# The end of a graph layer and LSTM kernel: last rows gated singly, sums on TensorE, the check between the output pieces

## The reference

```python
x = x + relu(adj @ (item @ W_item.T + b_item) + layernorm(x) @ W_user.T + b_user)   # adj 10000 x 10000
h = lstm(layernorm(x))                      # one sequence of 10000 steps, hidden size 128
g = argmax(h @ W_lin.T + b_lin, -1)         # 0 or 1 for every step
w = g * h
inc = cumsum(w, over steps); prefix = inc - w; suffix = inc[last] - inc
out = x + 2*h + prefix*fw_att + suffix*bw_att
```

## Time and profile before

| quantity | value |
|---|---|
| median of 3 runs | 1538.49 us (1537.8 to 1540.41) |
| profiled execution, its own time | 1538.81 us |
| its span | 1537.0 us |
| mean granted TensorE clock | 0.985 of full |
| busy TensorE / VectorE / ScalarE / GpSimd | 96% / 78% / 70% / 13% |
| DMA bytes | 426.73 MB |

### The profile page before, as it was taken

How to read it: one execution, slowest core, us unless ns; L and a number is a source line. 1 busy time by engine, 2 the same in 40 slices (tenths; PEclk the granted TensorE clock), 3 DMA queues, 4 the chain that set the end, 5 groups by cost and what they waited for, 6 DMA issues and landing times.

```text
span 1537.0 us, 25512 instructions
## 1 busy us (share of the span) xinstructions
PE 1471.3 (96%) x7890; PEld 1251.9 (81%) x7890; DVE 1201.8 (78%) x2018; ACT 1083.2 (70%) x1581; POOL 193.2 (13%) x172
## 2 busy tenths in 40 slices
PE   6999999999999999999999999999999899999991
PEld 5887887887887887887887887787787799999991
DVE  5998888888888888888888887887887456566667
ACT  4677777777777777777777777777776455556661
POOL 0000000000000000000000000000000000046765
PEclk9999999999999999999999999999999899999996
DMA  9789999999999999999999999999997300000003
GB/s 373 274 307 371 353 345 371 353 343 371 353 344 371 351 346 371 353 344 370 352 346 370 353 343 362 354 341 369 353 346 277 141 0 0 0 1 0 0 0 134
DMA packets 70080, 426.73 MB, mean 278 GB/s; under 512 B 8674, under 2 KB 17698, under 8 KB 69540
## 3 DMA queue, kind: packets, MB, share of 16 engines
q1 hardware_dynamic: 68320, 425.12, 73.1%
q10 hardware_dynamic: 1732, 1.24, 0.3%
HBM read 416.09 MB, written 10.24 MB: 277 GB/s over the span
## 4 chain that ended last, share of the span: by engine, by line
issue 77%; PE 20%; DVE 1%; POOL 0%; ACT 0%; POOLq 0%; DVEq 0%
PE psZ L729 9%; PE psZ L739 9%; PE psZ L745 1%; DVE y L1146 1%; POOL rstd L381 0%; POOLq L384 0%; DVE cum L1069 0%; ACT normed L492 0%; DVE cum L1067 0%; PE psV L639 0%; DVE dif L1057 0%; DVE dif L1054 0%; ACT u L506 0%; DVE y L1140 0%; DVE dif L1059 0%
## 5 line engine op out<-in xcount | busy, mean ns | idle before, releaser
L863 DVE TENSOR_TENSOR a_lo<-raw,a_hi 128x1000 fp32r<-128x1000 f32 (+1 forms) x800 | 907.4, 1180 | 139.6 <-ACT a_hi L521 136.1
L521 ACT ACTIVATE a_hi<-raw 128x1000 fp32r<-128x1000 f32 (+1 forms) x800 | 803.9, 1029 | 204.3 <-PE psG L664 185.6
L662 PE MATMUL psG<-a_hi,item_hi 128*128 128x500 f32 (+1 forms) x1580 | 637.0, 403 | 17.5 <-DVE a_lo L863 17.4
L664 PE MATMUL psG<-a_hi,item_lo 128*128 128x500 f32 (+1 forms) x1580 | 616.5, 390 | 0.0
L663 PE MATMUL psG<-a_lo,item_hi 128*128 128x500 f32 (+1 forms) x1580 | 613.6, 388 | 0.0
L662 PEld LDWEIGHTS psG<-a_hi,item_hi 128*128 128x128 f32 (+1 forms) x1580 | 297.0, 188 | 98.6 <-DVE a_lo L863 28.8
L664 PEld LDWEIGHTS psG<-a_hi,item_lo 128*128 128x128 f32 (+1 forms) x1580 | 298.1, 189 | 61.4
L663 PEld LDWEIGHTS psG<-a_lo,item_hi 128*128 128x128 f32 (+1 forms) x1580 | 298.0, 189 | 61.1 <-issue 4.4
L381 POOL TENSOR_TENSOR rstd<-var,minus_half 125x4 f32<-125x4 f32 x40 | 74.3, 1859 | 1119.4 <-DVE var L847 1119.4
L729 PE MATMUL psZ<-u,wx 128*128 (+1 forms) x1280 | 158.0, 277 | 1.6 <-POOL u L389 1.6
L729 PEld LDWEIGHTS psZ<-u,wx 128*128 128x128 f32 x1280 | 154.4, 194 | 3.6 <-issue 2.0
(11 more groups left out here) (111 smaller groups left out, 575.9 us busy)
## 6 DMA issues: line engine op xcount, KB each, us to landing
raw<-in_adj_main SPq DMA_DIRECT2D x360, 1000.0 KB, 5.7
raw<-in_adj_main SPq DMA_DIRECT2D x40, 750.0 KB, 4.1
x_copy<-xb SPq DMA_DIRECT2D x20, 250.0 KB, 5.2
x<-x_copy SPq DMA_DIRECT2D x1, 5000.0 KB, 15.5
out<-y SPq DMA_DIRECT2D x25, 200.0 KB, 2.4
xb<-in_xT SPq DMA_DIRECT2D x18, 250.0 KB, 5.4
u<-in_itemT SPq DMA_DIRECT2D x3, 1024.0 KB, 18.7
u<-in_itemT SPq DMA_DIRECT2D x1, 904.0 KB, 24.0
```

What stands on the lines that cost most here:

```text
L521: nc.scalar.activation(a_hi[:, s % CUT, 0:n], raw[:, r % RAW, at:at + n], ACT.Copy)\
L662: pe.matmul(bank, w_hi, hi, start=(c == 0), stop=False)
L664: last = pe.matmul(bank, w_lo, hi, start=False, stop=(c == CH))
L863: dve.tensor_tensor(a_lo[:, s % CUT, 0:n], raw[:, r % RAW, at:at + n], a_hi[:, s % CUT, 0:n].bitcast(f32), ALU.subtract).then_inc(lo_ready, 1)
```

## The change

The last pair of rows (38 and 39) is taken out of GpSimd's `sums`. Each of the two rows is gated by itself (`gate_row`). TensorE adds up, with identity and diagonal matrices as weights, what makes up their `y`: hist, x1 and dfb times the running sum, in PSUM banks 0 and 3; and in bank 1 the totals of every chunk (running sum before the pair plus the two gated rows). VectorE adds mbw times the gated row and writes the row of `y` (`last_y`). `cum` is made from the totals in PSUM. The shift is made twice: by VectorE into PSUM, which VectorE's pieces read, and by ScalarE into SBUF for GpSimd's. The check stands between piece 14 and piece 15 of the output; the head and piece 0 are last, and so is the store of piece 0; flag and branch come behind them. The branch now waits for all stores and writes the output anew from ScalarE's queue. A matrix `dfd` (dfb on the diagonal) is made once ahead of the LSTM.

```diff
-            for f in range(OUTS):                       # SyncE
+            for f in (*range(1, OUTS), 0):
...
-            with nc.gpsimd.Fori(PAIRS // 4 + 1, PAIRS // 2) as i:
+            with nc.gpsimd.Fori(PAIRS // 4 + 1, PAIRS // 2 - 1) as i:
                 sums(2 * i, 0)
                 sums(2 * i + 1, 1)
-            write_y(PAIRS - 1, 1)
-            pool.wait_ge(y_ready, PAIRS)
-            pool.wait_ge(shift_ready, 1)
+            sums(PAIRS - 2, 0)
+            pool.wait_ge(run_c_ready, PAIRS - 1)
+            write_y(PAIRS - 2, 0)
+            pool.wait_ge(y_ready, PAIRS - 1)
+            pool.wait_ge(last_rows, 2)
+            pool.wait_ge(shift_sb_ready, 1)
...
-            scale_gated(PAIRS - 1, 1)                   # ScalarE
-            scale_run(PAIRS - 1, 1)
+            act.wait_ge(total_ready, 1)
+            nc.scalar.activation(shift[:, :], cum[:, 0:K], ACT.Identity, scale=dfb[:, 0:1], bias=total[:, 0:1])
...
+            def add_up(w, columns, at, first=False, last=False):      # TensorE
+                return pe.matmul(psZ[:, SUM_BANK[at], 0:K], w[:, :], columns, start=first, stop=last, ...)
+            def add_total(columns, first=False, last=False):
+                return pe.matmul(psZ[:, TOT_BANK, 0:K], ident[:, :], columns, start=first, stop=last)
+            pe.wait_ge(t1_ready[0], STEPS)
+            pe.wait_ge(t1_ready[1], STEPS)
+            pe.wait_ge(run_ready, 2 * PAIRS - 1)
+            add_up(ident, hist[:, L - 2, :], 0, first=True)
+            add_total(run[:, 1, 0, :], first=True)
             pe.wait_ge(h_ready[0], STEPS)
             pe.wait_ge(h_ready[1], STEPS)
-            logits(L - 1, 1, 1)
+            pe.wait_ge(gated, PAIRS - 1)
+            logits(L - 1, 0, 0)
+            pe.wait_ge(gated, PAIRS)
+            add_total(gh[:, 1, 0, :])
+            pe.wait_ge(dfd_ready, 1)
+            add_up(dfd, run[:, 1, 0, :], 0)
+            add_up(ident, last_row(x1, L - 2), 0, last=True).then_inc(row_sums, 1)
+            pe.wait_ge(gated, PAIRS + 1)
+            add_total(gh[:, 1, 1, :], last=True).then_inc(totals, 1)
+            add_up(ident, hist[:, L - 1, :], 1, first=True)
+            add_up(dfd, run[:, 1, 0, :], 1)
+            add_up(dfd, gh[:, 1, 0, :], 1)
+            add_up(ident, last_row(x1, L - 1), 1, last=True).then_inc(row_sums, 1)
             pe.wait_ge(check, 5)
...
-            gate(PAIRS - 1, 1)                          # VectorE; the check followed here
+            gate_row(0)                                 # waits: d_ready L-1, run_ready, mgh_ready
+            dve.wait_ge(d_ready, L)
+            gate_row(1)
+            last_y(0)                                   # waits for row_sums 1
+            tot = psZ[:, TOT_BANK, :]
+            dve.wait_ge(totals, 1)
+            dve.tensor_tensor(cum[:, 0:1], tot[:, 1:2], cum[:, 1:2], ALU.add)
+            dve.tensor_tensor(cum[:, 2:3], tot[:, 0:1], cum[:, 0:1], ALU.add)
+            dve.tensor_tensor_scan(cum[:, 3:K + 1], tot[:, 2:K], hist[:, 0, 2:K], cum[:, 2:3], ALU.add, ALU.bypass)
+            last_y(1)                                   # waits for row_sums 2
+            dve.scalar_tensor_tensor(total[:, :], cum[:, K:K + 1], -1.0, mbw[:, :], ALU.mult, ALU.mult)
+            shift_ps = psZ[:, SHIFT_BANK, 0:K]
+            dve.tensor_scalar(shift_ps, cum[:, 0:K], dfb[:, 0:1], total[:, 0:1], ALU.mult, ALU.add)
+            for f in range(1, CHECK_AFTER):             # CHECK_AFTER = 15
+                if not by_pool(f):
+                    add_shift(f)                        # y piece + shift_ps
...                                                     # the check, unchanged
+            for f in range(CHECK_AFTER, OUTS):
+                if not by_pool(f):
+                    add_shift(f)
+            (the four pieces of the head, with shift_ps)
+            add_shift(0)
             dve.wait_ge(ok_sum, 1)
+            (flag, value_load, branch)
```

More of the change, by code:

```diff
@@ L67 @@
 D_BANK = (6, 7)
+SUM_BANK, TOT_BANK = (0, 3), 1
+SHIFT_BANK, OK_BANK = 4, 2
+CHECK_AFTER = 15
 AT = dict(relu=1, x1=2, bias=2, rows2=3, stats2=4, pair2=5, eps2=6, scale2=7, norm2=8, back2=9, out2=10,
@@ L178, in program @@
         shift = sb("shift", [P, K])
+        dfd = sb("dfd", [P, P])
         g_gt = sb("g_gt", [P, 4])
@@ L270, in program @@
         head_out = sem("head_out")
+        dfd_ready = sem("dfd_ready")
+        row_sums = sem("row_sums")
+        totals = sem("totals")
+        last_rows = sem("last_rows")
+        shift_sb_ready = sem("shift_sb_ready")
+        g_final = sem("g_final")
+        g_out_done = sem("g_out_done")
         out_done = sem("out_done")
@@ L287, in chunks_of, with last_row, shift_of @@
             return t[:, a * L:b * L].rearrange("p (k l) -> p k l", l=L)
-        def shift_of(a, b):
-            return shift[:, a:b].unsqueeze(2).to_broadcast([P, b - a, L])
+        def last_row(t, l):
+            return t[:, :].rearrange("p (k l) -> p k l", l=L)[:, :, l]
+        def shift_of(a, b, t=None):
+            return (shift if t is None else t)[:, a:b].unsqueeze(2).to_broadcast([P, b - a, L])
         def by_step(l0, l1, s0, s1):
@@ L611, in _ @@
             scale_run(PAIRS - 2, 0)
-            scale_gated(PAIRS - 1, 1)
-            scale_run(PAIRS - 1, 1)
+            act.wait_ge(total_ready, 1)
+            nc.scalar.activation(shift[:, :], cum[:, 0:K], ACT.Identity, scale=dfb[:, 0:1], bias=total[:, 0:1])\
+                .then_inc(shift_sb_ready, 1)
             act.wait_ge(flag_ready, 1)
@@ L622, in _ @@
                     nc.scalar.activation(g_tanh[:, :], g_C[:, :], ACT.Tanh, scale=0.5).then_inc(g_th, 1)
+                with nc.scalar.Fori(0, OUTS) as f:
+                    act.wait_ge(g_final, f + 1)
+                    act.dma_start(out[:, ds(f * OW, OW)], y[:, ds(f * OW, OW)]).then_inc(g_out_done, 16)
+                act.wait_ge(g_out_done, 16 * OUTS)
         @block.tensor
@@ L958, in _ @@
             dve.tensor_tensor(dfb[:, :], hfw[:, :], mbw[:, :], ALU.add).then_inc(dfb_ready, 1)
+            dve.wait_ge(dfb_ready, 1)
+            dve.tensor_scalar(dfd[:, :], ident[:, :], dfb[:, 0:1], None, ALU.mult).then_inc(dfd_ready, 1)
             dve.tensor_scalar(thr[:, :], thr0[:, :], 2.0, None, ALU.mult).then_inc(wd_ready, 1)
@@ L1045, in _, with gate_row, last_y @@
             lstm_pair(PAIRS - 2, 0)
-            gate(PAIRS - 1, 1)
+            def gate_row(half):
+                dve.scalar_tensor_tensor(gh[:, 1, half, :], psZ[:, D_BANK[1 - half], 0:K], thr[:, 0:1],
+                                         hist[:, L - 2 + half, :], ALU.is_gt, ALU.mult).then_inc(gated, 1)
+            def last_y(half):
+                dve.wait_ge(row_sums, half + 1)
+                dve.scalar_tensor_tensor(last_row(y, L - 2 + half), gh[:, 1, half, :], mbw[:, 0:1],
+                                         psZ[:, SUM_BANK[half], 0:K], ALU.mult, ALU.add)\
+                    .then_inc(last_rows, 1)
@@ new lines, in _ @@
+            dve.wait_ge(d_ready, L - 1)
+            dve.wait_ge(run_ready, 2 * PAIRS - 3)
+            dve.wait_ge(mgh_ready, PAIRS - 2)
+            gate_row(0)
[4 more added lines that the diff above has]
+            dve.wait_ge(totals, 1)
+            dve.wait_ge(cum_ready, 1)
+            dve.tensor_tensor(cum[:, 0:1], tot[:, 1:2], cum[:, 1:2], ALU.add).then_inc(cum_ready, 1)
+            dve.wait_ge(cum_ready, 2)
@@ new lines, in _ @@
+            dve.tensor_tensor(cum[:, 2:3], tot[:, 0:1], cum[:, 0:1], ALU.add).then_inc(cum_ready, 1)
+            dve.wait_ge(cum_ready, 3)
+            dve.tensor_tensor_scan(cum[:, 3:K + 1], tot[:, 2:K], hist[:, 0, 2:K], cum[:, 2:3], ALU.add, ALU.bypass)\
+                .then_inc(cum_ready, 1)
+            last_y(1)
+            dve.wait_ge(cum_ready, 4)
+            dve.scalar_tensor_tensor(total[:, :], cum[:, K:K + 1], -1.0, mbw[:, :], ALU.mult, ALU.mult)\
+                .then_inc(total_ready, 1)
@@ new lines, in _, with add_shift @@
+            dve.wait_ge(total_ready, 1)
+            shift_ps = psZ[:, SHIFT_BANK, 0:K]
+            dve.tensor_scalar(shift_ps, cum[:, 0:K], dfb[:, 0:1], total[:, 0:1], ALU.mult, ALU.add)\
+                .then_inc(shift_ready, 1)
+            dve.wait_ge(shift_ready, 1)
+            dve.wait_ge(y_ready, PAIRS - 1)
+            dve.wait_ge(last_rows, 2)
+            def add_shift(f):
+                a, b = max(f * OW // L, 3), (f + 1) * OW // L
+                dve.tensor_tensor(chunks_of(y, a, b), chunks_of(y, a, b), shift_of(a, b, shift_ps), ALU.add)\
+                    .then_inc(out_ready_v, 1)
@@ L1120, in _ @@
                 dve.wait_ge(g_out, 4 * NB + 1)
[L1121 to L1147, removed]
+                dve.scalar_tensor_tensor(total[:, :], g_cum[:, BW:BW + 1], -1.0, mbw[:, :], ALU.mult, ALU.mult)\
+                    .then_inc(g_end, 1)
+                dve.wait_ge(g_end, 1)
+                with nc.vector.Fori(0, OUTS) as f:
+                    rows = y[:, ds(f * OW, OW)]
```

(1 more changed line is left out.)

26 lines of the change are left out of this document (12 added, 14 removed).

## The result

| | before | after |
|---|---|---|
| median of the runs, us | 1537.80 (5 runs) | 1532.01 (1530.94 to 1532.61, 5 runs) |
| profiled execution / its span | 1538.81 / 1537.0 | 1532.61 / 1530.8 |
| start of the last state to the end of the span | 32.28 | 24.16 |

The ratio is 0.9958 (95% interval 0.9945 to 0.9971): 0.4% faster, 5.8 us in the medians. A second measurement of the same kernel gave 1531.45 against 1538.25 (0.9958, 0.9944 to 0.9971). The forecast was 1528.8 in a range up to 1532.0, so the direction was right, but the gain is 5.8 where 9.7 was forecast, and the time lies on the slow edge of the range (0.01 beyond it). The span was forecast at 1527.3 and came out at 1530.8.

What follows compares the result with a forecast made beforehand. Bound: last state to first store, then store flow. Piece 15 at 1519.16 + 0.8 pick-up + 5.93 for eleven stores + 1.4 gives span 1527.3; plus 1.81, less 0.3, median 1528.8; range 1526.8 to 1532.0.

Steps and rivals of the forecast that it cites:

- The bound: last state to first store, and the flow of stores: End of kernel: 15.2 us from last state to first store and 2.1 us lost in store flow can shrink.
- The first store at 1510.87, 6.15 behind the last state: Output stage: first store issues at about 1510.87 instead of 1519.94, 9.1 us earlier.
- A rule that speaks against it: 160-byte steps in TensorE's x1 reads and VectorE's y writes might cost 1.1 us; taken as nothing.
- rival 3: VectorE slower than taken: strides 1.1, held-up pieces up to 5, half clock 1.7; about 1530.5 to 1532; chance 0.24.
- Clock at its full level during the sums: TensorE's sums after the last logits run at 2.4 GHz; half level would add 1.7 us.
- Pieces at 0.49 free of GpSimd: VectorE's output pieces, reading the shift from PSUM, take 0.49 us each beside GpSimd; bounds 0.49 and 1.15.
- The check is late by 0.74: Between pieces 14 and 15 the check takes 3.89 us, so the next store's issue loses 0.74.
- Rival 1: The check takes 3.15 us or less and is hidden, stores run through; median 1528.1; chance 0.22.
- Piece 0, flag and branch at no cost: End: piece 0 is ready before SyncE needs it; flag and branch's 1.3 us lie beside the last stores.
- dfd at nothing: Ahead of the LSTM, making dfd fits in VectorE's idle 1.22 us: nothing, at most 0.1.
- Rival 2: Stores stay the limit in the old shape, first store no earlier; time about 1538; chance 0.03.
- rival 4: Slower than before: broadcast shift reads from PSUM slow all 17 VectorE pieces; at 1.15 each, median 1539.6; chance 0.04.

Runs made afterwards that it cites:

- late_check: Changed kernel with the check moved from behind piece 14 to behind piece 24; 1530.95 us, 0.9947 of the kernel before.
- x1_packed: Changed kernel with GpSimd copying rows 38 and 39 of x1 early into a packed tile that TensorE reads; 1530.76 us, 0.9949 of the kernel before.
- shift_sbuf: Changed kernel with VectorE's pieces reading the shift from SBUF (ScalarE's copy) instead of PSUM; 1534.58 us, 0.9975 of the kernel before.

## Why the prediction was right, and where it was off

- *The bound: last state to first store, and the flow of stores.* Right. 7.7 of the 8.1 us lie ahead of the first store, 0.4 behind it. The loss of 2.1 us in the flow was read too high: with no gap at all (late_check) the stores take 15.98 for 17.06, so 1.1 could be won.
- *The first store at 1510.87, 6.15 behind the last state.* It came at 7.50. The failed step is "A rule that speaks against it", where the strided reads of `x1` and writes of `y` are put at nothing: "I take nothing, because the fp32 matmul needs only one column in 1.7 ns". The two reads of `x1` cost 1.10: row sum 2 was read 5.56 behind the last state, and 4.46 with `x1` packed (x1_packed), for 4.57 forecast. That the row sum gates `total` was seen, so the whole delay of 0.99 went through. The other 0.36 lie on VectorE: 0.53 from last_y(1), which writes `y` at a step of 160 bytes, to `total`, instead of 0.37; 0.23 from `total` to `shift` instead of 0.20; 0.58 from `shift`, now into PSUM, to the first piece instead of 0.44; 0.60 from there to the store instead of 0.57. No run took these apart. The rows of ScalarE had shown the factor, and the bound of 1.1 that went into rival 3 was what happened. The Trainium skill (SBUF — State Buffer, section Door 1: The DMA port swizzle) had said that an access that crosses to a new 16-byte line pays a penalty; x1_packed agrees, with 3.8 ns a column against 1.7.
- *Clock at its full level during the sums.* Right: the granted clock was 1.00 from 1506 to 1512.3, and the other matmuls kept 0.58.
- *Pieces at 0.49 free of GpSimd.* Right (0.48), and shift_sbuf shows that the operand in PSUM is the reason.
- *The check is late by 0.74.* Right in kind; that the size came out near is partly luck. The check took 4.37 for 3.89, and the DMA lost 1.18 us to it, but the end only 0.66. Why it took longer than before was not tested; GpSimd's operations beside it were pieces instead of sums. Rival 1 (check hidden) would be reached at 3.15; alone it takes 2.5.
- *Piece 0, flag and branch at no cost.* Right: the flag at 1526.57, the last store issued at 1527.73.
- *dfd at nothing.* Nothing could be measured of it.
- *Rivals.* Rival 2 and rival 4 fell. Of rival 3 the strides came true beside the forecast's own mechanism, and the pieces held up by GpSimd did not; its price for those was fair (nine pieces up to 5 longer, 3.5 in the end; shift_sbuf: 5.33 and 3.6). Of the named signs of being wrong one showed: last_y(1) after 1509.8 (5.08 behind the last state; it came at 5.56).
- *The time.* The span was forecast at 1527.3 and came out at 1530.8: 1.6 from the steps above (24.16 for 22.6), 1.9 from the position of the last state. The prediction took the stage before as fixed; it moves by more than the error of all the steps together, and something like 1 us of it came with the new end. That the time still fell on the edge of the range owes nothing to rival 3's held-up pieces, which set that edge: strides and the earlier stage filled the same room.

## What to carry to other kernels

Where the chains of two engines end close together, removing one shows little (the check took 3.9, its removal gave 1.17); follow both to the same consumer before pricing one. An fp32 matmul whose moving columns lie 160 bytes apart ran at less than half speed, so a row used at the very end is worth packing earlier, on an engine with time. Putting one operand of a VectorE operation into PSUM freed it, and GpSimd, of each other: 3.6 us here for one changed operand.

## What the runs showed of the hardware that I had not expected

- The strided moving operand slows an fp32 matmul (0.95 for 250 columns, packed 0.42), although even packed a column takes 1.7 ns.
- One-column VectorE operations with two SBUF inputs took 1.06 to 1.41 beside a GpSimd operation; with one input in PSUM 0.16 to 0.18, beside GpSimd as well.
- A gap of 1.18 us in a queue of 25 stores cost only 0.66: without it 16 to 32 GB/s trickled on for 0.7 us behind the full rate, with it for 0.2.
